# Self attention of a perceiver block: a loop of four heads at a time, or sixteen heads written out with scores three heads ahead

## The chip, the cores and the metric

The kernel runs on one core of one Trainium2 chip, in one launch. The metric is the device time of the whole kernel in microseconds (us), the median of several executions. Engines are named as the profile names them: PE is TensorE's matrix multiplication and PEld its weight load, DVE is VectorE, ACT is ScalarE, POOL is GpSimd, SP is SyncE, which here only issues DMAs.

## The reference, cut to what matters

The whole program is two layers of cross attention, self attention and a feed forward part. The change touches only one piece, the self attention inside the first layer's cross attention block: 256 tokens, 16 query heads of 128, and 8 groups of keys and values, so that two neighbouring query heads share one group. In the reference's own words:

```python
def _gqa(q, k, v):
    scale = 1.0 / np.sqrt(q.shape[-1])
    scores = jnp.einsum('bsghd,btgd->bghst', q, k) * scale
    p = jax.nn.softmax(scores, axis=-1)
    return jnp.einsum('bghst,btgd->bsghd', p, v)
```

The result is divided by a smoothing vector and clipped to the range of fp8 before it goes on to the output projection.

## The kernel before

The kernel is a row of stages. Each stage is one block in which every engine runs its own list of instructions, ordered against the others by semaphores, and every stage ends with a barrier of all engines. `front_stage` computes queries, keys and values, `self_attention_stage` (line 166) is the one that is changed, and `wide_cross_attention_stage` (line 285) follows it. The queries `qT` [128 dims, 16 heads, 256 tokens], keys `kT` [128, 8, 256] and values `v` [128 tokens, 2, 8 x 128] lie in SBUF when the stage begins. All are fp32.

The stage before is a hardware loop of four passes; a pass takes two groups, which is four heads (n = 0 to 3). Per head the work is:

- PE: scores, two products of 128x256 (line 226), then four transposes of 128x128 of the probabilities (line 233), then the weighing of the values, two products of 128x256 into `out` (line 217, function `weigh`). The profile has two records for each fp32 product, so scores and weighing have four records of 128x256 each, and the transposes four of 128x128.
- DVE: the row peaks of the scores (`tensor_reduce`, line 267), the shift (line 268); later the reciprocal of the row sums (line 271) and two multiplications that normalise `prob` (lines 272 and 273); for each group of two heads the outputs are scaled (line 278) and clipped into `cat` (line 280).
- ACT: two exponentials with their sums (line 250), and later the copy of the transposed probabilities out of PSUM (line 255).
- POOL: for each group it copies the queries, keys and values to `q`, `k`, `val` (lines 202 to 204); PE's scores wait for that copy (`s_in`).

A pass runs phase by phase: PE makes the scores of all four heads; DVE finds the four peaks, then normalises the four; ACT makes all eight exponentials, then the four copies; PE turns head n and then weighs head n-1; DVE puts the two groups away at the end. `scores` and `prob` have four buffers each, `tp` two, `out` two. `Chain.after` (called `link`) makes an engine wait until the instruction just issued has completed; it stands behind the first multiplication (line 272) and behind the clipping (line 280) as well.

SP issues five loads for the next stage at the start of this one (lines 3079 and 3081); PE first waits for them in the next stage.

Of the kernel before, what the change touches and what calls it, by code (L numbers as in the profile page):

```python
# [31 lines left out]
NH = 16  # L32
NG = 8
EPS = 1e-5
FP8_MAX = 448.0
# [129 lines left out]

def self_attention_stage(nc, C, qT, kT, v, inv_smooth, cat, loads):

    scale = D**-0.5
    with Stage(nc, "self") as st:
        q = [st.sb(f"q{e}", [P, 2, TOK]) for e in range(2)]
        k = [st.sb(f"k{e}", [P, TOK]) for e in range(2)]
        val = [st.sb(f"val{e}", [P, NT, D]) for e in range(2)]
# [10 lines left out]
        names = "free staged scores shift exp norm turned probT out put dve"  # L186
        s_free, s_in, s_sc, s_sh, s_exp, s_norm, s_tp, s_pt, s_out, s_put, s_dve = (st.sem(n) for n in names.split())
        with nc.Block() as block:

            @block.sync  # L190
            def _(sp):
                loads(sp)

            @block.gpsimd
            def _(pool):

                with pool.Fori(0, NG // 2) as i:
                    for e in range(2):
                        pool.wait_ge(s_out, i * 4 + (2 * e + 2))
                        pool.sem_inc(s_free, 1)  # L200
                        pool.wait_ge(s_free, i * 2 + (e + 1))
                        pool.tensor_copy(q[e][:, :, :], qT[:, bass.ds(i * 4 + 2 * e, 2), :]).then_inc(s_in, 1)
                        pool.tensor_copy(k[e][:, :], kT[:, bass.ds(i * 2 + e, 1), :].rearrange("p a n -> p (a n)")).then_inc(s_in, 1)
                        pool.tensor_copy(val[e][:, :, :], v[:, :, bass.ds(i * (2 * D) + e * D, D)]).then_inc(s_in, 1)

            @block.tensor
            def _(pe):
                pe.sem_inc(s_out, 4)
                pe.sem_inc(s_tp, 4)
                with pe.Fori(0, NG // 2) as i:  # L210
                    def weigh(n):
                        e, u = n // 2, n % 2
                        pe.wait_ge(s_pt, i * 4 + (n + 5))
                        if u == 0:
                            pe.wait_ge(s_put, i * 2 + (e + 1))
                        for kt in range(NT):
                            mm = pe.matmul(out[e][:, u, :], val[e][:, kt, :], probT[n][:, kt, :], start=(kt == 0), stop=(kt == 1))
                        mm.then_inc(s_out, 1)

                    for n in range(4):  # L220
                        e, u = n // 2, n % 2
                        if u == 0:
                            pe.wait_ge(s_in, i * 6 + (3 * e + 3))
                        pe.wait_ge(s_exp, i * 8 + (2 * n + 2))
                        for t in range(NT):
                            mm = pe.matmul(scores[n][:, t, :], q[e][:, u, t * P:(t + 1) * P], k[e][:, :], start=True, stop=True)
                        mm.then_inc(s_sc, 1)
                    for n in range(4):
                        pe.wait_ge(s_norm, i * 4 + (n + 5))
                        pe.wait_ge(s_pt, i * 4 + (n + 3))  # L230
                        for t in range(NT):
                            for kt in range(NT):
                                mm = pe.transpose(tp[n % 2][:, kt, t * P:(t + 1) * P], prob[n][:, t, kt * P:(kt + 1) * P],
                                                  C["ident"][:, :])
                        mm.then_inc(s_tp, 1)
                        if n >= 1:
                            weigh(n - 1)
                    weigh(3)

            @block.scalar  # L240
            def _(act):
                act.sem_inc(s_exp, 8)
                act.sem_inc(s_pt, 4)
                with act.Fori(0, NG // 2) as i:
                    for n in range(4):
                        act.wait_ge(s_tp, i * 4 + (n + 1))
                        act.wait_ge(s_norm, i * 4 + (n + 1))
                        act.wait_ge(s_sh, i * 4 + (n + 1))
                        for t in range(NT):
                            act.activation(prob[n][:, t, :], scores[n][:, t, :], ACT.Exp, bias=shift[:, n, t:t + 1],  # L250
                                           scale=scale, accum_out=total[:, n, t:t + 1]).then_inc(s_exp, 1)
                    for n in range(4):
                        act.wait_ge(s_tp, i * 4 + (n + 5))
                        act.wait_ge(s_out, i * 4 + (n + 1))
                        act.copy(probT[n][:, :, :], tp[n % 2][:, :, :]).then_inc(s_pt, 1)

            @block.vector
            def _(dve):
                PER = 4 * 3 + 2 * 2
                dve.sem_inc(s_norm, 4)  # L260
                dve.sem_inc(s_put, 2)
                with dve.Fori(0, NG // 2) as i:
                    chain = Chain(dve, s_dve, i * PER)
                    link = chain.after
                    for n in range(4):
                        dve.wait_ge(s_sc, i * 4 + (n + 1))
                        link(dve.tensor_reduce(peak[:, n, :], scores[n][:, :, :], AX.X, ALU.max))
                        dve.tensor_scalar(shift[:, n, :], peak[:, n, :], -scale, None, ALU.mult).then_inc(s_sh, 1)
                    for n in range(4):
                        dve.wait_ge(s_exp, i * 8 + (2 * n + 10))  # L270
                        link(dve.reciprocal(inv[:, n, :], total[:, n, :]))
                        link(dve.tensor_scalar(prob[n][:, 0, :], prob[n][:, 0, :], inv[:, n, 0:1], None, ALU.mult))
                        dve.tensor_scalar(prob[n][:, 1, :], prob[n][:, 1, :], inv[:, n, 1:2], None, ALU.mult) \
                           .then_inc(s_norm, 1)
                    for e in range(2):
                        heads = bass.ds(i * 4 + 2 * e, 2)
                        dve.wait_ge(s_out, i * 4 + (2 * e + 6))
                        link(dve.tensor_tensor(scaled[e][:, :, :], out[e][:, :, :],
                                               inv_smooth[:, heads].unsqueeze(2).to_broadcast([P, 2, TOK]), ALU.mult))
                        link(dve.tensor_scalar(cat[:, heads, :], scaled[e][:, :, :], FP8_MAX, -FP8_MAX, ALU.min, ALU.max))  # L280
                        dve.sem_inc(s_put, 1)
                    assert chain.n == PER, chain.n


def wide_cross_attention_stage(nc, C, ctxT, s_ctx, w, s_w, wkv_dram, q_dram, vecs, inv_smooth, cat, units, early):
# [2818 lines left out]
```

## Time and profile before

| | us |
|---|---|
| median of 3 runs | 2563.33 (2561.7 to 2565.37) |
| the profiled execution's own time | 2560.87 |
| its span, first to last instruction | 2559.1 |
| self attention stage, first load issued to last output put | 131.27 to 193.98 |

The span is what the trace covers; the 1.8 us between it and the execution's time lie around it. The stage is 62.7 us, some 2.4% of the span. The mean granted TensorE clock over the whole execution is 0.959 of full speed.

### The profile page before, as it was taken

Reading aid. Unit: us, or ns where it says so; the run is one execution under the profiler, and the core shown is the slowest. Engines: PE = TensorE matmul, PEld = TensorE weight load, DVE = VectorE, ACT = ScalarE, POOL = GpSimd, SP = SyncE. Lnnn points to the kernel's source line nnn. Section 1 sums busy time; section 2 is a strip of 40 time slices with the busy share of each in tenths; the row PEclk is TensorE's granted clock in tenths of the full one; section 3 lists DMA queues with packets and bytes.
Section 4 is the critical chain, followed back from the end, with each engine's and each line's share of the span. In section 5 each row is a group of like instructions: output and inputs, shape, how many; then the busy total and the mean of one; then the engine's idle time right before and its main releaser. Section 6 shows DMA issues by size and latency. Waiting matters only on the chain. (4 is left out here: it accounts for less than half of the span.)

```text
span 2559.1 us, 31520 instructions
## 1 busy us (share of the span) xinstructions
PE 2279.3 (89%) x11472; PEld 1554.3 (61%) x11472; DVE 1786.6 (70%) x3422; ACT 1193.7 (47%) x1924; POOL 587.4 (23%) x435
## 2 busy tenths in 40 slices
PE   3779999999999999896897989788888779899998
PEld 2556666666666666564674456555556337677876
DVE  7856887777777778876896976666767754554444
ACT  4443466666566666633332114576766853211111
POOL 7810033334233333440000003323141300000000
PEclk9889999999999999998997999999999989899999
DMA  3331100000000100003544100000000013656661
GB/s 132 116 140 46 46 25 29 9 29 9 29 25 13 29 13 17 0 1 132 193 169 188 52 21 10 1 10 1 6 5 1 21 75 144 216 206 220 230 237 66
DMA packets 47622, 186.40 MB, mean 73 GB/s; under 512 B 6064, under 2 KB 10928, under 8 KB 37232
## 3 DMA queue, kind: packets, MB, share of 16 engines
q1 hardware_dynamic: 47472, 184.43, 20.0%
q8 instruction: 91, 1.49, 0.2%
q14 instruction: 59, 0.48, 0.1%
HBM read 174.71 MB, written 9.70 MB: 72 GB/s over the span
## 5 line engine op out<-in xcount | busy, mean ns | idle before, releaser
L406 PE MATMUL wide_a<-wide_w,ctxT 128*128 128x256 f32 (+1 forms) x2048 | 437.8, 367 | 2.8 <-POOL wide_eps L375 2.8
L406 PEld LDWEIGHTS wide_a<-wide_w,ctxT 128*128 128x128 f32 x2048 | 368.5, 191 | 76.5 <-issue 35.7
L388 POOL TENSOR_TENSOR wide_sums<-wide_sums,wide_s 128x512 f32<-128x512 f32 x224 | 301.3, 1345 | 461.8 <-ACT wide_s L536 448.6
L431 PE MATMUL wide_scores<-wide_q,wide_keysT 128*128 128x512 f32 x512 | 238.4, 604 | 12.5 <-ACT wide_s L532 12.5
L441 PE MATMUL wide_o<-wide_s,wide_values 128*128 128x512 f32 x512 | 233.8, 600 | 3.5 <-ACT wide_s L536 3.5
L532 ACT COPY wide_s<-wide_scores 128x512 f32<-128x512 f32 x256 | 148.4, 585 | 175.7 <-PE wide_scores L431 173.9
L1812 DVE TENSOR_REDUCE int_peaks<-int_a 128x1 f32<-128x1024 f32 x128 | 156.1, 1222 | 91.3 <-PE int_a L1535 90.1
L1535 PE MATMUL int_a<-int_keys,int_qrows 96*128 96x512 bf16 x512 | 151.8, 394 | 55.9 <-DVE int_peaks L1812 27.9
L1687 ACT ACTIVATE int_prob<-int_a,int_shift,int_qscale 128x1024 uint8<-128x1024 f32 x128 | 155.4, 1216 | 50.6 <-PE int_a L1535 50.1
L431 PEld LDWEIGHTS wide_scores<-wide_q,wide_keysT 128*128 128x128 f32 x512 | 87.9, 189 | 148.8 <-ACT wide_s L532 87.8
L594 DVE TENSOR_TENSOR wide_top<-wide_top,wide_s 128x512 f32<-128x512 f32 x240 | 165.6, 690 | 16.1 <-ACT wide_s L532 10.4
L2268 PEld LDWEIGHTS moe_bank<-moe_xb,moe_gate_up 128*128 128x128 f32 (+1 forms) x1536 | 162.0, 183 | 8.3 <-issue 8.3
L2268 PE MATMUL moe_bank<-moe_xb,moe_gate_up 128*128 128x96 f32 (+1 forms) x1536 | 162.6, 266 | 4.3 <-issue 4.3
L441 PEld LDWEIGHTS wide_o<-wide_s,wide_values 128*128 128x128 f32 x512 | 96.7, 192 | 100.2 <-issue 93.9
L607 DVE TENSOR_TENSOR wide_s<-wide_s,wide_peak_rows 128x2048 f32<-128x2048 f32 x64 | 146.8, 2294 | 0.8
L570 DVE BATCH_NORM_STATS2 wide_stats<-wide_keys 128x6 f32<-128x128 f32 x256 | 60.6, 278 | 110.9 <-ACT wide_values L514 108.4
L1446 PE MATMUL int_vp<-int_wk,ctxT_again 128*128 128x128 f32 x1024 | 126.6, 279 | 5.2 <-PEq L79 2.2
L1446 PEld LDWEIGHTS int_vp<-int_wk,ctxT_again 128*128 128x128 f32 x1024 | 122.7, 194 | 12.3 <-issue 4.0
L512 ACT COPY wide_keys<-wide_a 128x256 f32<-128x256 f32 x128 | 46.6, 364 | 174.3 <-PE wide_a L406 174.2
L536 ACT ACTIVATE wide_s<-wide_s 128x2048 f32<-128x2048 f32 x64 | 122.4, 1912 | 5.5 <-DVE wide_s L607 4.8
L1535 PEld LDWEIGHTS int_a<-int_keys,int_qrows 96*128 96x128 bf16 x512 | 37.0, 99 | 118.8 <-DVE int_peaks L1812 49.7
L2469 DVE TENSOR_REDUCE moe_coef<-moe_misc 96x1 f32<-96x4 f32 x32 | 5.1, 158 | 137.3 <-PE moe_misc L2277 137.3
(425 smaller groups left out, 4285.7 us busy)
## 6 DMA issues: line engine op xcount, KB each, us to landing
moe_gate_up<-hbm_m_gu SPq DMA_DIRECT2D x34, 1408.0 KB, 6.2
moe_down<-hbm_m_down_a SPq DMA_DIRECT2D x34, 512.0 KB, 6.9
causal_wqkv<-hbm_wqkv SPq DMA_DIRECT2D x8, 1536.0 KB, 6.6
ctxT<-hbm_ctxT SPq DMA_DIRECT2D x4, 2048.0 KB, 15.1
oproj_raw<-hbm_wproj SPq DMA_DIRECT2D x8, 1024.0 KB, 5.0
ctxT_again<-hbm_ctxT SPq DMA_DIRECT2D x4, 2048.0 KB, 21.6
wide_unit<-hbm_ffn_units SPq DMA_DIRECT2D x27, 256.0 KB, 2.7
ffn_early<-wide_unit SPq DMA_DIRECT2D x27, 256.0 KB, 2.0
```

Source lines behind the costliest of these rows:

```text
L388: ins = pool.tensor_tensor(sums[0][:, :], before, part[:, j, :], ALU.add)
L406: mm = pe.matmul(a[h][:, j, cols], ctxT[:, kc, t * P:(t + 1) * P], w[g % 2][:, kc, cols], start=(kc == 0), stop=(kc == KC - 1))
L431: pe.matmul(sp_[j % 2][:, :], keysT[:, j, :], q[:, :], start=True, stop=True).then_inc(s_s, 1)
L441: mm = pe.matmul(o[g % 2][:, :], values[m % VR][:, j, :], s[m % SR][:, j, :], start=(c == 0 and j == 0), stop=(c == QPG - 1 and j == 3))
L532: act.copy(s[n % SR][:, j, :], sp_[j % 2][:, :]).then_inc(s_se, 1)
L594: link(dve.tensor_tensor(top[:, :], before, s[n % SR][:, j, :], ALU.max))
L607: dve.tensor_tensor(s[m % SR][:, :, :], s[m % SR][:, :, :], peak_rows[:, :].unsqueeze(1).to_broadcast([P, 4, COLS]), ALU.subtract).then_in ...
L1446: mm = pe.matmul(vp[:, t * P:(t + 1) * P], ctxT[:, kc, i * P:(i + 1) * P], wk[:, kc, :], start=(kc == 0), stop=(kc == KC - 1))
L1535: mm = pe.matmul(wide[n % 2][:, z * 512:(z + 1) * 512], qrows[0:3 * HD, h, t * P:(t + 1) * P], keys[0:3 * HD, h % HC, j * 512:(j + 1) * 51 ...
L1687: act.activation(prob[u % 4][:, p * 1024:(p + 1) * 1024], wide[n % 2][:, :], ACT.Exp, bias=shift[:, u % NU:u % NU + 1], scale=qscale[:, t, ...
L1812: dve.tensor_reduce(peaks[u % 2][:, p:p + 1], wide[n % 2][:, :], AX.X, ALU.max).then_inc(s_ad, 1)
L2268: mm = pe.matmul(dst[0:m, j, :], wgu[i][:, kc, z * EI + f0:z * EI + f0 + m], xb[q % 2][:, kc, e % BATCH, :], start=(kc == 0), stop=(kc == ...
```

## The change

The loop is gone: the sixteen heads are written out (n = 0 to 15), each with its own instructions, so that PE reads `qT`, `kT` and `v` where they are. POOL has no work in the stage. The order on the engines is another one. `AHEAD` is 3: the scores, peaks and exponentials of heads 0 to 2 come first, and then sixteen steps follow. In step n PE turns head n, makes the scores of head n+3 and weighs head n-1; ACT copies the turned head n and makes the exponentials of head n+3; DVE normalises head n, finds the peaks of head n+3, and in every second step from n = 3 puts one group away. Buffers are the same in number. The waits behind the first multiplication and behind the clipping are gone.

```diff
             @block.tensor
             def _(pe):
...
+                for n in range(AHEAD):
+                    score(n)
+                for n in range(NH):
+                    turn(n)
+                    if n + AHEAD < NH:
+                        score(n + AHEAD)
+                    if n >= 1:
+                        weigh(n - 1)
+                weigh(NH - 1)
...
+                def score(n):
+                    if n >= 4:
+                        pe.wait_ge(s_exp, 2 * (n - 3))
+                    for t in range(NT):
+                        mm = pe.matmul(scores[n % 4][:, t, :], qT[:, n, t * P:(t + 1) * P], kT[:, n // 2, :], start=True, stop=True)
+                    mm.then_inc(s_sc, 1)
+
+                def turn(n):
+                    pe.wait_ge(s_norm, n + 1)
+                    if n >= 2:
+                        pe.wait_ge(s_pt, n - 1)
...
+                def weigh(n):
+                    g, u = divmod(n, 2)
+                    pe.wait_ge(s_pt, n + 1)
+                    if u == 0 and g >= 2:
+                        pe.wait_ge(s_put, g - 1)
+                    for kt in range(NT):
+                        mm = pe.matmul(out[g % 2][:, u, :], v[:, kt, g * D:(g + 1) * D], probT[n % 4][:, kt, :],
+                                       start=(kt == 0), stop=(kt == NT - 1))
+                    mm.then_inc(s_out, 1)
...
             @block.scalar
             def _(act):
...
+                for n in range(AHEAD):
+                    exponential(n)
+                for n in range(NH):
+                    keep_turned(n)
+                    if n + AHEAD < NH:
+                        exponential(n + AHEAD)
...
             @block.vector
             def _(dve):
...
+                def find_peak(n):
+                    dve.wait_ge(s_sc, n + 1)
+                    link(dve.tensor_reduce(peak[:, n % 4, :], scores[n % 4][:, :, :], AX.X, ALU.max))
+                    dve.tensor_scalar(shift[:, n % 4, :], peak[:, n % 4, :], -scale, None, ALU.mult).then_inc(s_sh, 1)
+
+                def normalise(n):
+                    dve.wait_ge(s_exp, 2 * n + 2)
+                    link(dve.reciprocal(inv[:, n % 4, :], total[:, n % 4, :]))
+                    dve.tensor_scalar(prob[n % 4][:, 0, :], prob[n % 4][:, 0, :], inv[:, n % 4, 0:1], None, ALU.mult)
+                    dve.tensor_scalar(prob[n % 4][:, 1, :], prob[n % 4][:, 1, :], inv[:, n % 4, 1:2], None, ALU.mult).then_inc(s_norm, 1)
+
+                def put(g):
+                    heads = slice(2 * g, 2 * g + 2)
+                    dve.wait_ge(s_out, 2 * g + 2)
+                    link(dve.tensor_tensor(scaled[g % 2][:, :, :], out[g % 2][:, :, :],
+                                           inv_smooth[:, heads].unsqueeze(2).to_broadcast([P, 2, TOK]), ALU.mult))
+                    dve.tensor_scalar(cat[:, heads, :], scaled[g % 2][:, :, :], FP8_MAX, -FP8_MAX, ALU.min, ALU.max).then_inc(s_put, 1)
+
+                for n in range(AHEAD):
+                    find_peak(n)
+                for n in range(NH):
+                    normalise(n)
+                    if n + AHEAD < NH:
+                        find_peak(n + AHEAD)
+                    if n >= 3 and n % 2 == 1:
+                        put((n - 3) // 2)
+                put(NG - 1)
```

## Rows read from the trace of the kernel before

**Rows 1.** Windows, a pass each: length; PE, PEld, DVE, ACT, POOL busy; clock; DMA share; GB/s
```profile
131.30:146.00 14.70, 10.02 (x51) 8.02 (x52) 8.08 (x23) 7.17 (x21) 4.03 (x10) 1.00 0.94 389
146.00:161.60 15.60, 12.58 (x50) 9.53 (x49) 9.14 (x25) 7.22 (x21) 2.98 (x6) 0.78 0.48 205
161.60:177.20 15.60, 11.95 (x47) 9.21 (x46) 9.00 (x24) 7.17 (x21) 2.98 (x6) 0.78 0.00 1
177.20:194.00 16.80, 11.68 (x50) 8.70 (x48) 10.12 (x26) 7.17 (x21) 1.49 (x3) 0.90 0.00 0
```

**Rows 2.** Waits within 131.3 to 194.1 us: waiter, releaser, total us, times, longest
```profile
ACT L250 <- DVE self_shift L268: 17.9, 4, 4.9
...
PE self_tp L233 <- DVE self_prob L273: 10.3, 7, 2.6
...
PE self_scores L226 <- POOL self_val L204: 4.1, 4, 3.5
```

**Rows 3.** Timeline of the first pass: start us, us, engine, line, operation, idle before
```profile
131.27 0.33 SPq L3079 DMA_DIRECT2D wide_w<-hbm_wkvx  x1
...
133.19 3.72 PE L226 MATMUL self_scores<-self_k,self_q 128*128 128x256 f32 x16 [3.48 <-POOL self_val L204]
...
134.35 0.69 DVE L267 TENSOR_REDUCE self_peak<-self_scores 128x2 f32<-128x512 f32 x1 [9.54 <-PE self_scores L226]
135.08 0.17 DVE L268 TENSOR_SCALAR self_shift<-self_peak 128x2 f32<-128x2 f32 x1
...
135.35 1.28 ACT L250 ACT_TABLE_LOAD   x1 [4.92 <-DVE self_shift L268]
...
137.67 0.17 DVE L268 TENSOR_SCALAR self_shift<-self_peak 128x2 f32<-128x2 f32 x1
137.77 0.17 DVE L271 RECIPROCAL self_inv<-self_total 128x2 f32<-128x2 f32 x1
...
137.97 0.35 DVE L272 TENSOR_SCALAR self_prob<-self_prob,self_inv 128x256 f32<-128x256 f32 x1
...
138.36 0.35 DVE L273 TENSOR_SCALAR self_prob<-self_prob,self_inv 128x256 f32<-128x256 f32 x1
...
138.85 0.65 PE L233 MATMUL self_tp<-ident,self_prob 128*128 128x128 f32 x4 [1.94 <-DVE self_prob L273]
```

**Rows 4.** Timeline later in that pass, and the outputs put away beside it
```profile
142.40 1.03 PE L217 MATMUL self_out<-self_probT,self_val 128*128 128x256 f32 x4
...
143.27 0.60 PE L233 MATMUL self_tp<-ident,self_prob 128*128 128x128 f32 x4
...
143.70 1.97 PE L217 MATMUL self_out<-self_probT,self_val 128*128 128x256 f32 x8
...
145.81 0.69 DVE L278 TENSOR_TENSOR self_scaled_out<-self_out,inv_smooth 128x512 f32<-128x512 f32 x1 [0.80 <-PE self_out L217]
...
146.65 0.58 DVE L280 TENSOR_SCALAR cat<-self_scaled_out 128x512 f32 x1 [0.15 <-DVE self_scaled_out L278]
```

**Rows 5.** Timeline of the second pass, behind its idle stretch on PE
```profile
152.19 2.02 PE L233 MATMUL self_tp<-ident,self_prob 128*128 128x128 f32 x8 [2.58 <-DVE self_prob L273]
...
154.42 2.07 PE L217 MATMUL self_out<-self_probT,self_val 128*128 128x256 f32 x4 [0.21 <-ACT self_probT L255]
...
156.28 1.06 PE L233 MATMUL self_tp<-ident,self_prob 128*128 128x128 f32 x4
...
157.14 1.92 PE L217 MATMUL self_out<-self_probT,self_val 128*128 128x256 f32 x4
```

**Rows 6.** Timeline: the last output, and the first products of the next stage
```profile
193.55 0.43 DVE L280 TENSOR_SCALAR cat<-self_scaled_out 128x512 f32 x1 [0.15 <-DVE self_scaled_out L278]
...
195.34 9.91 PE L406 MATMUL wide_a<-wide_w,ctxT 128*128 128x256 f32 x37 [2.77 <-POOL wide_eps L375]
```

**Rows 7.** Timeline, next stage: four multiplications with no wait between them
```profile
214.06 1.12 DVE L582 TENSOR_SCALAR wide_keys<-wide_keys,wide_mv,wide_rstd 128x128 f32<-128x128 f32 x4
```

**Rows 8.** Groups by line, VectorE, 205 to 330 us: busy, mean ns, idle before
```profile
L582 DVE TENSOR_SCALAR wide_keys<-wide_keys,wide_mv,wide_rstd 128x128 f32<-128x128 f32 x44 | 12.3, 341 | 0.4
```

More of the change, by code:

```diff
@@ L171, in self_attention_stage @@
     scale = D**-0.5
+    AHEAD = 3
     with Stage(nc, "self") as st:
-        q = [st.sb(f"q{e}", [P, 2, TOK]) for e in range(2)]
-        k = [st.sb(f"k{e}", [P, TOK]) for e in range(2)]
-        val = [st.sb(f"val{e}", [P, NT, D]) for e in range(2)]
         prob = [st.sb(f"prob{n}", [P, NT, TOK]) for n in range(4)]
@@ L185, in self_attention_stage @@
         out = [st.ps(f"out{e}", [P, 2, TOK]) for e in range(2)]
-        names = "free staged scores shift exp norm turned probT out put dve"
-        s_free, s_in, s_sc, s_sh, s_exp, s_norm, s_tp, s_pt, s_out, s_put, s_dve = (st.sem(n) for n in names.split())
+        names = "scores shift exp norm turned probT out put dve"
+        s_sc, s_sh, s_exp, s_norm, s_tp, s_pt, s_out, s_put, s_dve = (st.sem(n) for n in names.split())
         with nc.Block() as block:
@@ L192, in _ @@
                 loads(sp)
[L194 to L204, printed above, removed]
@@ L206, in _ @@
             @block.tensor
             def _(pe):
[L208 to L215, printed above, removed]
-                        for kt in range(NT):
[L217 to L238, printed above, removed]
@@ new lines, in score @@
+                def score(n):
[8 more added lines that the diff above has]
+                        pe.wait_ge(s_pt, n - 1)
+                    for t in range(NT):
+                        for kt in range(NT):
+                            mm = pe.transpose(tp[n % 2][:, kt, t * P:(t + 1) * P], prob[n % 4][:, t, kt * P:(kt + 1) * P],
+                                              C["ident"][:, :])
+                    mm.then_inc(s_tp, 1)
@@ L240, in _, with exponential @@
+                for n in range(NH):
[5 more added lines that the diff above has]
+                weigh(NH - 1)
             @block.scalar
             def _(act):
[L242 to L255, printed above, removed]
+                def exponential(n):
+                    act.wait_ge(s_sh, n + 1)
+                    if n >= 4:
+                        act.wait_ge(s_tp, n - 3)
+                    for t in range(NT):
+                        act.activation(prob[n % 4][:, t, :], scores[n % 4][:, t, :], ACT.Exp, bias=shift[:, n % 4, t:t + 1],
+                                       scale=scale, accum_out=total[:, n % 4, t:t + 1]).then_inc(s_exp, 1)
@@ L257, in _, with keep_turned @@
+                def keep_turned(n):
+                    act.wait_ge(s_tp, n + 1)
+                    if n >= 4:
+                        act.wait_ge(s_out, n - 3)
+                    act.copy(probT[n % 4][:, :, :], tp[n % 2][:, :, :]).then_inc(s_pt, 1)
+                for n in range(AHEAD):
[4 more added lines that the diff above has]
+                        exponential(n + AHEAD)
             @block.vector
@@ L258, in _ @@
             def _(dve):
[L259 to L282, printed above, removed]
@@ new lines, in _ @@
+                link = Chain(dve, s_dve).after
+                def find_peak(n):
[7 more added lines that the diff above has]
+                    dve.tensor_scalar(prob[n % 4][:, 1, :], prob[n % 4][:, 1, :], inv[:, n % 4, 1:2], None, ALU.mult).then_inc(s_norm, 1)
```

## The prediction

> **What bounds the kernel now.** Only one stage of 62.7 us changes, from the first load at 131.27 [rows 3] to the last output's end at 193.55 + 0.43 = 193.98 [rows 6]; everything else can only be shifted. First I read the windows, one for each pass of the loop [rows 1]: in none of the four is an engine busy all the time (PE 10.0 to 12.6 us of passes of 14.7 to 16.8 us, DVE 8.1 to 10.1, ACT 7.2). So no engine is the bound; a chain of waits through all of them is. Then the waits [rows 2]: ACT waits 17.9 us for the first shift of each pass, PE 10.3 us for normalised probabilities, PE 4.1 us for GpSimd's copies. The timeline of the first pass shows the chain [rows 3]: scores at 133.19, the first peak at 134.35, the shift at 135.08, then a table load of 1.28 us on ACT behind it, the exponentials, the reciprocal at 137.77, two multiplications, and the first transposes at 138.85, PE having idled for 1.94 us. Later in the pass PE runs dense: four records of weighing, then four transposes 0.87 us later, then the next weighing 0.43 us later [rows 4]. The clock column [rows 1] is 1.00 in the first pass, 0.78, 0.78 and 0.90 in the others. With two levels, 2.4 and 1.2 GHz, that is (1 - 0.78) x 2 x 15.6 = 6.9 us at the low one, again 6.9, and (1 - 0.90) x 2 x 16.8 = 3.4, 5.7 on the mean. The falls lie around the idle stretch before the transposes, 2.58 us in the second pass [rows 5] (this row stands for three, of 2.55 to 2.58), not around the 1.94 us of the first [rows 3]. PE also idled 2.77 us at the border to the next stage [rows 6].
>
> **What the change removes.** GpSimd's copies: scores can start at the stage's start, about 131.5 (I take 0.2 behind the first load at 131.27) in place of 133.19, 1.7 us earlier, and the smaller waits for later copies go, 0.2 each. Three of four table loads should go, as one load served both exponentials and copies within a pass and the list is now one; each stood between a shift and an exponential [rows 3], 3 x 1.28 = 3.8 us. The borders between passes go, where PE has no softmax work to turn. These gains aren't added to anything below: the new stage is summed from its start, and they are inside it.
>
> **What it adds: a closed loop through PE and DVE.** Read the new lists in order. DVE: normalise(n), peak(n+3), normalise(n+1). PE: turn(n), score(n+3), weigh(n-1). turn(n) waits for normalise(n); score(n+3) is queued behind it on PE; peak(n+3) waits for the scores; normalise(n+1) is queued behind the peak on DVE. So though the exponentials are three heads ahead, no step can be shorter than this round:
> - end of normalising to first transpose 0.14 (138.36 + 0.35 to 138.85 [rows 3])
> - transposes to what follows on PE 0.43 (143.27 to 143.70 [rows 4])
> - start of the scores to start of the peak 1.16 (133.19 to 134.35 [rows 3])
> - peak to shift 0.73, shift to reciprocal 0.10, reciprocal to first multiplication 0.20 [rows 3]
> - first multiplication to second: 0.39 before, with a wait between them [rows 3]. The wait is gone. Four multiplications of half the size with no wait take 1.12 us [rows 7] where one takes 0.341 [rows 8], so the next starts (1.12 - 0.341) / 3 = 0.26 after the one before, 0.08 less than its length. The same here: 0.35 - 0.08 = 0.27, call it 0.28. Bounds: 0.28 and 0.39
> - second multiplication 0.35 [rows 3]
>
> Sum 3.39 us. In every second step from n = 3 a put stands between peak(n+3) and normalise(n+1): 0.84 from scaling to clipping (145.81 to 146.65), and the clipping, 0.58 beside GpSimd's copies [rows 4] and 0.43 without them [rows 6], less the overlap of 0.08: about 1.20. A long step is 4.59. ACT, with 7.2 / 4 = 1.8 us a head [rows 1], and PE's weighing, 0.87 [rows 4], fit under either. The Trainium skill speaks on the wait taken out: "VectorE: DVE Perf Modes", section "The DRAIN you can't avoid", says that leaving semaphores out between VectorE operations saves nothing. By that each step would be 0.11 longer, 1.4 us over 13 steps; rows 7 and 8 show the overlap, and I go by them.
>
> **The sum.** From score(0) at 131.5 to the first reciprocal it takes what it took, 137.77 - 133.19 = 4.58, the one table load in it: 136.1. Thirteen steps (n = 0 to 12) have the round: 13 x 3.39 = 44.1, and five puts among them (n = 3, 5, 7, 9, 11) add 6.0: 186.2. The tail has no scores: normalise(13) 0.83, put 1.20, normalise(14) 0.83, normalise(15) meanwhile; turn(14) starts at 189.2 and ends its 0.43, weigh(13) 0.87, turn(15) 0.43, to 190.9; the copy of head 15 runs to 191.8 beside weigh(14); weigh(15) 1.03 to 192.9; 0.13 more, then put(7), 0.84 + 0.43: the end at 194.3. Before it was 193.98. At full clock the change is worth +0.3 us: the borders, copies and loads saved are spent again on the round, (13 x 3.39 + 6.0) / 13 = 3.9 us a head, the same as the 15.6 / 4 = 3.9 of a pass [rows 1].
>
> **The clock on top.** In a short step PE works 0.43 + 0.87 + 0.87 = 2.17 and idles 1.2 us; in a long one it idles 2.4. That is between the 1.94 us that left the clock up and the 2.55 that brought it down each time, and there are five long steps. At the low level the transposes' 0.43 becomes 0.86 (156.28 to 157.14 [rows 5]) and the scores' four records 2.07 [rows 5] in place of 1.03 [rows 4]; both lie in the round, so a step is 1.47 longer, 4.86. A fall that holds 5.7 us, the mean of before, costs 5.7 x 1.47 / 4.86 = 1.7 us. Before, falls met short transposes alone behind the idle stretch; here 2.17 us of work follow each gap, so I take two falls of five: 3.4. Total +3.7 us. Bounds: none, and all steps low, 13 x 1.47 = 19.1.
>
> **At nothing.** SP's five loads for the next stage are issued as before, now with no wait of PE for them until the next stage; its first product is at 195.34 [rows 6]. Reading `qT`, `kT`, `v` in place: same shapes and types, 0. Straight code on PE is four times as long as the loop's body and is fetched while those loads fill the DMA engines (share 0.94 [rows 1]); nothing here shows a price, I bound it by 0 and by one step, 3.4, and take 0. Weighing one head later is covered: its copy of 0.6 us is made long before.
>
> **Rivals.**
> A (forecast): few falls of the clock, +3.7: the profiled execution's 2560.87 becomes 2564.6, and the median, 2563.33 or 2.46 above it, 2567.0. Own range +1.5 to +6.
> B: the clock falls at each long step. 5 x 1.7 = 8.6, plus 0.3: +8.9, 2572.2. For it: the gaps of 2.4 us, near 2.55. Against: in pass one, gap 1.94, nothing fell. The Trainium skill, "Perfetto Trace Analysis", section "Matmul Optimizations", would have this rival: the engine scales its power by use, so matmuls should run back to back in batches, and the change spreads batches of eight and sixteen into small ones. The trace bears it out only where idle stretches were over 2.5 us.
> C: no fall; the new stage is as long as the old, +0.3: 2563.6. The pipeline is there, but the round eats it.
> D (the other side): the round is not closed, that is, DVE finds the scores of head n+3 ready whenever it comes to them. Then DVE is free of the 0.14 + 0.43 + 1.16, and PE's own 2.17 or DVE's 0.73 + 0.10 + 0.83 + 0.60 (half a put) = 2.26 binds: 13 x (3.85 - 2.26) = 20.7 us less, 2543. It needs scores issued ahead of the wait for normalise(n), and the list has them behind it. It decides from a saving of 5.4 / 13 = 0.4 us a step.
>
> **The numbers.** 0.2% of 2563 is 5.1 us, about what a measurement of this kernel can tell from no change. A 0.50, B 0.25, C 0.17, D 0.08. Slower by over 0.2%: nearly all of B (0.23) and the upper end of A (0.05), 0.28. Faster: 0.07 from D. Within: 0.65. The range is 2561 to 2573: C's lower side (if the fixed hops are some 0.2 us shorter a step) to just above B; it leaves out D and the steps all at low clock. The time is A's, 2567.0; A's own range is 2564.8 to 2569.3.
>
> **What would show it.** In the profile after: DVE waiting for scores (line of the peak) 13 times, 1.7 us or so each, and PE waiting for the normalised probabilities 13 times; starts of the peaks 3.4 and 4.6 us apart by turns; one table load in the stage; no GpSimd work; the clock between 0.85 and 1.00. Wrong if the peaks come 2.3 us apart (D), if PE waits for nothing between steps, if steps at full clock are not near 3.39, or if the clock is under 0.8 (B).

## The result, and the profile after

The changed kernel takes 2552.63 us (median of 9 runs, 2550.07 to 2554.79) where the kernel before takes 2561.7 (9 runs): a ratio of 0.9970, 95% interval 0.9959 to 0.9981, some 7.7 us or 0.3% faster. One of the nine executions of the kernel before took 9195.4 us and is left out of the ratio, which goes by the median of the other eight, 2560.4. The forecast was 2567.0 in 2561 to 2573, no measurable change most likely. The time lies below the range and the sign of the likeliest case was wrong.

The page of the changed kernel begins:

```profile
span 2550.8 us, 31191 instructions
...
PE 2268.6 (89%) x11472; PEld 1546.6 (61%) x11472; DVE 1783.5 (70%) x3422; ACT 1191.7 (47%) x1921; POOL 575.8 (23%) x411
```

The windows of the stage in four stretches, columns as in [rows 1]; the stage runs from 130.08 to 189.40 us:

```profile
130.08:145.00 14.92, 9.79 (x49) 7.60 (x50) 7.83 (x24) 8.94 (x28) 0.00 (x0) 1.00 0.95 392
145.00:160.00 15.00, 9.51 (x49) 7.29 (x49) 8.22 (x24) 6.42 (x20) 0.00 (x0) 1.00 0.49 206
160.00:175.00 15.00, 10.50 (x45) 7.64 (x43) 8.13 (x24) 6.00 (x19) 0.00 (x0) 0.89 0.00 1
175.00:189.40 14.40, 10.05 (x52) 7.63 (x52) 8.84 (x25) 5.40 (x15) 0.00 (x0) 1.00 0.00 0
```

GpSimd is idle, and the clock is down in one stretch only: (1 - 0.89) x 2 x 15.0 = 3.3 us, against 6.9 + 6.9 + 3.4 in [rows 1]. PE's busy time for the same 192 records fell from 46.2 to 39.9 us, mostly for that reason. The stage fell from 62.71 to 59.32 us. The waits within it (in the form of [rows 2]):

```profile
DVE self_peak L257 <- PE self_scores L195: 29.4, 14, 7.7
...
PE self_tp L204 <- DVE self_prob L264: 18.2, 14, 1.9
ACT self_prob L235 <- DVE self_shift L258: 17.2, 14, 1.9
```

This is the closed round: VectorE waited 14 times for scores, PE 14 times for normalised probabilities; the three heads of lead take nothing off this round. The start of the stage, which answers to [rows 3]:

```profile
130.08 0.33 SPq L3078 DMA_DIRECT2D wide_w<-hbm_wkvx  x1
130.08 1.28 ACT L235 ACT_TABLE_LOAD   x1 [0.85 <-PEq L79]
...
130.12 2.83 PE L195 MATMUL self_scores<-kT,qT 128*128 128x256 f32 x12 [1.61 <-PEq L79]
...
131.26 0.69 DVE L257 TENSOR_REDUCE self_peak<-self_scores 128x2 f32<-128x512 f32 x1 [7.66 <-PE self_scores L195]
...
133.71 0.17 DVE L258 TENSOR_SCALAR self_shift<-self_peak 128x2 f32<-128x2 f32 x1
133.79 0.16 DVE L262 RECIPROCAL self_inv<-self_total 128x2 f32<-128x2 f32 x1
```

The table load now lies at the very start, before ACT waits for the first shift. VectorE finds three peaks in front of the first reciprocal, where the loop has four [rows 3], and the reciprocal is 3.67 us behind the first score, not 4.58. One step with a put, from the turning of head 3 to that of head 4 (it answers to [rows 3, 4]):

```profile
144.33 0.65 PE L204 MATMUL self_tp<-ident,self_prob 128*128 128x128 f32 x4 [0.84 <-DVE self_prob L264]
...
144.82 1.03 PE L195 MATMUL self_scores<-kT,qT 128*128 128x256 f32 x4
...
145.89 0.69 DVE L257 TENSOR_REDUCE self_peak<-self_scores 128x2 f32<-128x512 f32 x1 [1.61 <-PE self_scores L195]
146.62 0.17 DVE L258 TENSOR_SCALAR self_shift<-self_peak 128x2 f32<-128x2 f32 x1
146.69 0.68 DVE L269 TENSOR_TENSOR self_scaled_out<-self_out,inv_smooth 128x512 f32<-128x512 f32 x1
```

```profile
147.41 0.43 DVE L271 TENSOR_SCALAR cat<-self_scaled_out 128x512 bf16<-128x512 f32 x1
147.75 0.16 DVE L262 RECIPROCAL self_inv<-self_total 128x2 f32<-128x2 f32 x1
147.95 0.35 DVE L263 TENSOR_SCALAR self_prob<-self_prob,self_inv 128x256 f32<-128x256 f32 x1
148.22 0.35 DVE L264 TENSOR_SCALAR self_prob<-self_prob,self_inv 128x256 f32<-128x256 f32 x1
```

```profile
148.62 0.66 PE L204 MATMUL self_tp<-ident,self_prob 128*128 128x128 f32 x4 [1.90 <-DVE self_prob L264]
```

The first and the last of these three fences are the timeline of all engines, the middle one that of VectorE alone, which keeps the clipping apart. The step is 148.62 - 144.33 = 4.29 us; without a put it is 3.23 (peaks at 136.21, 139.44, 142.66 and 145.89).

### The profile page after: what moved, and what is told of

It is laid out like the page before. It is cut to its first block and busy times, and to the rows that moved or that the text cites. A ratio compares the mean times of both kernels' runs of the same rounds, so it can differ in the third digit from the quotient of the medians.

```text
span 2550.8 us, 31191 instructions
## 1 busy us (share of the span) xinstructions
PE 2268.6 (89%) x11472; PEld 1546.6 (61%) x11472; DVE 1783.5 (70%) x3422; ACT 1191.7 (47%) x1921; POOL 575.8 (23%) x411
## 5 line engine op out<-in xcount | busy, mean ns | idle before, releaser
L1445 PEld LDWEIGHTS int_vp<-int_wk,ctxT_again 128*128 128x128 f32 x1024 | 124.0, 195 | 13.1 <-issue 4.3
## 6 DMA issues: line engine op xcount, KB each, us to landing
ctxT_again<-hbm_ctxT SPq DMA_DIRECT2D x4, 2048.0 KB, 20.7
```

Source lines behind the costliest of these rows:

```text
L1445: mm = pe.matmul(vp[:, t * P:(t + 1) * P], ctxT[:, kc, i * P:(i + 1) * P], wk[:, kc, :], start=(kc == 0), stop=(kc == KC - 1))
```

## The experiments

"Stage" is from the first load of the stage to the end of its last output in the profiled execution, as 62.71 us before. "Clock" is the granted clock's mean in that stretch. Each ratio from control on is to executions of the kernel before taken beside it (medians 2559.76 to 2560.1). Below, a "hop" is the time from one engine's work to the work on another that waited for it.

| kernel | median us | ratio to before, 95% interval | stage us | clock |
|---|---|---|---|---|
| before | 2561.7 | | 62.71 | 0.86 |
| changed | 2552.63 | 0.9970 (0.9959 to 0.9981) | 59.32 | 0.97 |
| control | 2559.80 | 0.9997 (0.9987 to 1.0007) | 64.91 | 0.79 |
| before_third | 2556.00 | 0.9991 (0.9976 to 1.0005) | 63.87 | 0.81 |
| after_again | 2551.61 | 0.9971 (0.9960 to 0.9981) | 59.32 | 0.97 |
| u_place | 2547.49 | 0.9952 (0.9938 to 0.9967) | 52.84 | 0.90 |
| u_pool | 2549.44 | 0.9958 (0.9945 to 0.9972) | 57.79 | 0.85 |
| loop_warm | 2554.47 | 0.9980 (0.9970 to 0.9990) | 58.30 | 0.88 |
| links | 2554.47 | 0.9980 (0.9971 to 0.9988) | 63.63 | 0.95 |
| ahead2 | 2554.64 | 0.9985 (0.9973 to 0.9996) | 61.27 | 0.97 |
| put_early | 2544.84 | 0.9951 (0.9934 to 0.9968) | 53.26 | 1.00 |
| open_loop | 2538.34 | 0.9913 (0.9899 to 0.9928) | 42.46 | 1.00 |
| open_put_early | 2530.62 | 0.9890 (0.9874 to 0.9907) | 38.92 | 1.00 |
| u_place_long | 2552.20 | 0.9972 (0.9960 to 0.9983) | 58.22 with the added copies | 0.89 |

**control: the kernel before, unchanged.**

> The kernel before, run again and profiled once more, to see what its profile repeats. Theory 1 (the gain outside the stage is chance: TensorE's clock falls at other places from run to run): the stage from first load to last output is again 61 to 64 us, while the stages before and after it differ from the first profile by one to several us, about as much as the changed kernel's did (1.2 us before the stage, some 3.6 us after it). Theory 2 (the change shortens other stages as well): the rest of the kernel repeats within 0.5 us. Ratio to the kernel before 1.000, within 0.2%, by both.

The stage took 64.91 us. In front of it nothing changed (first load at 131.20, 131.27 before); behind it, from the next stage's first product to the end, it took 2562.0 - 197.47 = 2364.5 us, 2363.8 before, 0.7 apart. This one profile nearly fits the second theory, so the question went on to before_third and u_place_long.

**u_place: the old order, written out, read in place.** Each `Fori` becomes a Python loop, and GpSimd's block goes.

```diff
-                with pe.Fori(0, NG // 2) as i:
+                for i in range(NG // 2):
...
-                            mm = pe.matmul(scores[n][:, t, :], q[e][:, u, t * P:(t + 1) * P], k[e][:, :], start=True, stop=True)
+                            mm = pe.matmul(scores[n][:, t, :], qT[:, 4 * i + n, t * P:(t + 1) * P], kT[:, 2 * i + e, :], start=True, stop=True)
```

> The old order, phase by phase in passes of four heads, but written out without a loop, with constant waits, and with queries, keys and values read in place. Theory 1 (what gained is the loop's disappearance: table loads inside it, register arithmetic and waits against registers, GpSimd's copies): the stage falls to 50 to 57 us from 62.7, as much as or more than the change's 59.3, and the whole kernel is 5 to 12 us faster than before. Theory 2 (the new order gained, through less idle TensorE and a clock that stays up): the stage stays at 60 us or more and the kernel is within 3 us of before.

The stage fell to 52.84 us, 6.5 below the changed kernel's, and the kernel is 12.3 us faster than before against the change's 7.7 (its slowest execution, 2549.55, is below the changed kernel's fastest, 2550.07). So the new order did not bring the gain: writing out and reading in place did, and the new order gave part of it back. The windows of the whole stage:

```profile
129.77:182.61 52.84, 42.22 (x192) 33.51 (x192) 34.32 (x96) 25.45 (x81) 0.00 (x0) 0.90 0.41 170
```

And one hop of it from VectorE to PE, normalising to turning:

```profile
148.67 0.35 DVE L256 TENSOR_SCALAR self_prob<-self_prob,self_inv 128x256 f32<-128x256 f32 x1
...
149.08 0.66 PE L216 MATMUL self_tp<-ident,self_prob 128*128 128x128 f32 x4 [2.06 <-DVE self_prob L256]
```

From 148.67 + 0.35 = 149.02 to 149.08 is 0.06 us, where the loop has 0.14 [rows 3]. The same is seen in u_pool, and the scaling of an output is 0.73 us ahead of its clipping in both, 0.84 in the loop [rows 4]; loop_warm, which keeps the loop, keeps 0.13 and 0.84. The work is the same in u_pool, so these two places cost 0.08 and 0.11 us more in the loop. That registers in its waits and addresses are what costs is likely, but no run separates it.

**u_pool: the same, GpSimd's copies kept.**

> The kernel before, written out without a loop, with constant waits, but GpSimd still copies queries, keys and values. Theory (the loop itself costs, the copies only at their start and a little in each pass): the stage is 54 to 56 us, 1.5 to 3 us above u_place's 52.8. Rival (the copies are what cost, the loop is free): the stage stays at 60 us or more, 7 us or more above u_place.

57.79 us, 4.9 above u_place, more than expected. 3.05 us of it is the start: PE, kept waiting for the first copies, began 1.3 us later, and the clock fell 1.1 us behind its start, for 3.4 us.

```profile
132.10 5.41 PE L226 MATMUL self_scores<-self_k,self_q 128*128 128x256 f32 x16 [3.24 <-POOL self_val L204]
```

Sixteen records of scores took 5.41 us, 3.72 in [rows 3]; the first reciprocal came 7.92 us behind the first load, 4.87 in u_place. The passes afterwards are as long as u_place's (the first reciprocals of two passes are 13.1 to 13.5 us apart in both). Another 1.7 us came behind the last of these, where the clock fell once more and in u_place did not. Against before, writing out alone gave 10.7 us of kernel time, of which the profiled stages show 6.0 against the mean of before's three (63.8).

**loop_warm: the loop kept, the table load moved.**

```diff
                 with act.Fori(0, NG // 2) as i:
+                    act.activation(warm[:, :], C["ident"][:, 0:1], ACT.Exp)
```

> The kernel before with its loop, and one exponential of a single column of the identity into an unused tile at the start of each pass on ACT, so that the table load is done while ACT has nothing else to do, not between the first shift and the first exponential. Theory (the load of 1.28 us stands on the path of each pass, and the idle stretch of TensorE that it lengthens brings the clock down): the load leaves the path, 4 x 1.28 = 5 us off the stage of 62.7 to 64.9, and the idle stretches of 2.55 us before the first transposes of a pass become 1.3, so that the clock falls less often, 1 to 3 us more. Rival (the load is hidden behind something else): no change.

```profile
145.06 1.28 ACT L246 ACT_TABLE_LOAD   x1
146.36 0.20 ACT L246 ACTIVATE self_warm<-ident 128x1 f32<-128x1 f32 x1
149.34 0.47 ACT L252 ACTIVATE self_prob<-self_scores,self_shift 128x256 f32<-128x256 f32 x1 [2.78 <-DVE self_shift L270]
```

The load lies behind the copies of the pass before. The stage is 58.30 us and the kernel 5.1 us faster (interval 2.6 to 7.7): one small instruction in the old loop brings two thirds of what the whole change brought. But the load did not cost its 1.28 us in each pass, as expected. First reciprocals of the first two passes here, a stretch at full clock:

```profile
139.08 0.17 DVE L273 RECIPROCAL self_inv<-self_total 128x2 f32<-128x2 f32 x1
...
151.63 0.17 DVE L273 RECIPROCAL self_inv<-self_total 128x2 f32<-128x2 f32 x1
```

The pass took 12.55 us, against 13.35 at full clock in the kernel before (137.77 [rows 3] to 151.12): 0.80 us, 3.2 over four passes, which is an estimate. The first reciprocal of a pass did not come earlier; in both kernels it stands right behind the fourth shift, 5.56 and 5.61 us behind the second pass's first scores. What came earlier is what follows the exponentials on ACT: in the first pass the first copy of turned probabilities started 0.69 us behind the start of its transposes, not 1.40, and PE's weighing waits for it. The other 1.2 of the 4.4 us between the two profiled stages are not traced; the clock was 0.88 here, 0.86 there. The second half of the expectation failed too: PE's idle stretches were still 1.94 and 2.50 to 2.54 us.

**links: the two waits put back.**

```diff
-                    dve.tensor_scalar(prob[n % 4][:, 0, :], prob[n % 4][:, 0, :], inv[:, n % 4, 0:1], None, ALU.mult)
+                    link(dve.tensor_scalar(prob[n % 4][:, 0, :], prob[n % 4][:, 0, :], inv[:, n % 4, 0:1], None, ALU.mult))
```

(and the same behind the clipping, which then signals by an instruction of its own, as before the change)

> The changed kernel with the two waits put back, behind the first normalising multiplication and behind the clipping. Theory (the trace's overlap of VectorE instructions with no wait between them is real): each step is 0.12 us longer (second multiplication 0.39 behind the first, not 0.27) and each of the puts 0.1 to 0.15, in all 2 to 2.5 us on a stage of 59.3. Rival (leaving such waits out saves nothing): the steps stay at 3.23 and 4.29.

VectorE's timeline in a step with a put:

```profile
144.86 0.35 DVE L263 TENSOR_SCALAR self_prob<-self_prob,self_inv 128x256 f32<-128x256 f32 x1
145.25 0.35 DVE L264 TENSOR_SCALAR self_prob<-self_prob,self_inv 128x256 f32<-128x256 f32 x1
...
148.74 0.43 DVE L271 TENSOR_SCALAR cat<-self_scaled_out 128x512 bf16<-128x512 f32 x1
149.31 0.17 DVE L262 RECIPROCAL self_inv<-self_total 128x2 f32<-128x2 f32 x1
```

The multiplications are 0.39 us apart, 0.27 without the wait, and the reciprocal 0.57 behind the clipping, 0.34 without it (147.41 to 147.75 above). Steps are 3.35 and 4.64 us at full clock: over thirteen steps with five puts 13 x 0.12 + 5 x 0.23 = 2.7 us. The kernel is 2.4 us slower than the mean of the changed one's two medians (2552.1), though the two intervals overlap; the timeline is the firmer evidence. The profiled stage, 63.63, also has one fall of the clock more in it than the changed kernel's.

**ahead2: AHEAD = 2.**

> The changed kernel with scores, peaks and exponentials two heads ahead in place of three. Theory of the closed round: how far ahead the scores are makes no difference to a step, it is 3.23 us again; there is one more step with scores (14) and one head fewer in front of them, so the stage is within 2 us of the changed kernel's. Rival (the distance hides ACT's exponentials and matters): steps become longer by a good part of the two exponentials, 0.5 us or more each, and the kernel 6 us or more slower than the changed one.

```profile
135.87 0.69 DVE L257 TENSOR_REDUCE self_peak<-self_scores 128x2 f32<-128x512 f32 x1 [1.61 <-PE self_scores L195]
...
139.09 0.69 DVE L257 TENSOR_REDUCE self_peak<-self_scores 128x2 f32<-128x512 f32 x1 [1.61 <-PE self_scores L195]
```

Steps are 3.23 us again and the stage 61.27, 2.0 above. The lead of three heads does not set the step. With two peaks in front of the first reciprocal it came 3.12 us behind the first score, and waited 0.22 us for an exponential.

**open_loop: scores ahead of the turning.**

```diff
                 for n in range(NH):
-                    turn(n)
                     if n + AHEAD < NH:
                         score(n + AHEAD)
+                    turn(n)
```

> The changed kernel with one edit: in each step TensorE issues the scores of head n+3 before it turns head n, so they no longer stand behind the wait for normalise(n). Theory of the closed round (as in the prediction): VectorE no longer waits for scores, steps fall from 3.23 and 4.29 us to TensorE's own work, about 2.25 on the mean, so the 13 steps take 29 to 31 us in place of 48, the stage 41 to 45 us, and the kernel is 14 to 18 us faster than the changed one. Rival (the steps are bound by something else, ACT's exponentials or VectorE's own work with its latencies): steps stay above 3 us on the mean and the gain is under 4 us.

The stage fell by 16.9 us to 42.46 and the kernel by 13.8 below the changed kernel's mean median, a little less than expected. Two steps take 5.15 us together, 2.58 each, not 2.25. Why not less shows in the timeline:

```profile
150.95 0.69 DVE L257 TENSOR_REDUCE self_peak<-self_scores 128x2 f32<-128x512 f32 x1 [0.96 <-PE self_scores L195]
...
151.75 0.68 DVE L269 TENSOR_TENSOR self_scaled_out<-self_out,inv_smooth 128x512 f32<-128x512 f32 x1
...
153.68 0.66 PE L204 MATMUL self_tp<-ident,self_prob 128*128 128x128 f32 x4 [0.60 <-DVE self_prob L264]
```

In the step with a put VectorE first waits 0.96 us for scores, then does the put, and PE waits 0.60 us for the probabilities behind it.

**put_early: the put ahead of the peaks.**

```diff
                     normalise(n)
+                    if n >= 3 and n % 2 == 1:
+                        put((n - 3) // 2)
                     if n + AHEAD < NH:
                         find_peak(n + AHEAD)
-                    if n >= 3 and n % 2 == 1:
-                        put((n - 3) // 2)
```

> The changed kernel with one edit: in the steps that have a put, VectorE does it before it looks for the peaks of head n+3, not after. Theory of the closed round: VectorE waits 1.6 us for those scores in each step anyway, the put of 1.06 us goes into that wait, and all steps are 3.23 us; the five long steps of 4.29 vanish, which takes 5 us off the stage (59.3 to 54) and off the kernel. Rival (VectorE's own work is the bound): the order of its work makes no difference, steps stay 3.23 and 4.29.

```profile
141.51 0.69 DVE L257 TENSOR_REDUCE self_peak<-self_scores 128x2 f32<-128x512 f32 x1 [1.62 <-PE self_scores L195]
...
143.03 0.68 DVE L269 TENSOR_TENSOR self_scaled_out<-self_out,inv_smooth 128x512 f32<-128x512 f32 x1
143.75 0.43 DVE L271 TENSOR_SCALAR cat<-self_scaled_out 128x512 bf16<-128x512 f32 x1
144.73 0.69 DVE L257 TENSOR_REDUCE self_peak<-self_scores 128x2 f32<-128x512 f32 x1 [0.56 <-PE self_scores L195]
...
147.96 0.69 DVE L257 TENSOR_REDUCE self_peak<-self_scores 128x2 f32<-128x512 f32 x1 [1.61 <-PE self_scores L195]
```

The put lies in the wait, 0.56 us of which is left; every step is 3.23 us, also the one with the put. The stage is 53.26 us and the kernel 7.3 us below the changed kernel's mean median. Swapping two calls on VectorE is worth as much as the whole change.

**open_put_early: both.**

> Both edits: scores of head n+3 before the turning of head n on TensorE, and the put before the peaks on VectorE. In open_loop a pair of steps takes 5.15 us, and in it VectorE still waits 0.96 us for scores, while its put makes TensorE wait for normalised probabilities. Theory: the put fills that wait, and a pair comes down to TensorE's own work, 2 x 2.2 = 4.4 us; the stage falls from 42.5 to 38 or 39 us, the kernel by 3 to 4 us below open_loop. Rival (the latencies from peaks through exponentials to the normalising bind now): the pair stays at 5.15.

```profile
128.85:167.77 38.92, 36.35 (x192) 29.68 (x192) 32.45 (x96) 26.02 (x81) 0.00 (x0) 1.00 0.56 230
```

PE is busy 36.35 of 38.92 us at full clock. Steps are 2.58 and 1.75 or 1.92 us, a pair 4.33 to 4.50: now PE is the bound. The stage fell by 3.5 us below open_loop's, as expected; the kernel's medians differ by 7.7, more than expected, from five executions each. The kernel is 2530.62 us, 1.1% (0.9 to 1.3%) faster than before and the fastest of all, 21 us ahead of the change.

**after_again and before_third.**

> The changed kernel once more, for a second profile and time. Theory (the fixed hops decide, the clock adds by chance): at full clock the steps are again 3.23 and 4.29 us to 0.02, and what differs is the number of falls of the clock in the stage, 0 to 4, each some 0.8 to 1.5 us; the stage is 58.6 to 64 us and the kernel 5 to 9 us faster than before. Rival (the first profile's single fall is a property of this order): the stage is again 59.3 within 0.3.

> The kernel before, profiled a third time, for the spread of its stages. The stage 61 to 65 us, the stages behind it 2363 to 2366 us if the difference to the written out kernels is a property of the kernel; anywhere in 2357 to 2366 if it is chance.

The changed kernel's stage was 59.32 us once more, with one fall of 3.4 us at another place; its steps at full clock were 3.23 and 4.29. It is what the rival had said; but links and ahead2, with the same order, had two falls and one, so how many come is not settled by two equal profiles. The kernel before had 63.87 us, and behind the stage 2554.1 - 195.80 = 2358.3 us, among what the written out kernels showed. So the stages behind differ by 6 us from one execution to another of one program.

**u_place_long.**

```diff
+                for r in range(12):
+                    link(dve.tensor_copy(scaled[0][:, :, :], scaled[1][:, :, :]))
```

> u_place with twelve copies of 128x512 on VectorE behind its last output, each waited for, about 0.6 to 0.8 us each: nothing of it is used, it only makes the stage as long as the looped kernel's. The stages behind the self attention took 2363.7 to 2366.0 us in three looped profiles and 2357.1 to 2362.3 in seven written out. Theory (that is the time of day: the later stages meet other falls of TensorE's clock when they start earlier): with the stage 7 to 10 us longer they take 2363 to 2366 again, and the kernel is 3 us or more slower than u_place plus the added stage time. Rival (it is the code: straight lists in place of loops change something that lasts): they stay at 2357 to 2362, and the kernel is u_place's time plus the added stage time.

A copy took 0.46 us, so the stage grew by only 5.6 us, from 52.58 without the copies. The kernel became 4.7 us slower, no more than the added time, and behind the stage it took 2550.9 - 189.88 = 2361.0 us. That speaks against the theory of the starting time, weakly, since the added time was smaller than meant. The same profile has a pass of the old order, written out, at full clock:

```profile
136.91 0.16 DVE L254 RECIPROCAL self_inv<-self_total 128x2 f32<-128x2 f32 x1
...
148.43 0.16 DVE L254 RECIPROCAL self_inv<-self_total 128x2 f32<-128x2 f32 x1
```

It took 11.52 us, 2.88 us a head.

## Why the prediction was wrong

**Right: the round.** PE and VectorE form one closed chain, at full clock every step has the length of that chain, a step with a put is longer by the put, and the lead of three heads hides nothing of it. open_loop and put_early, each an exchange of two calls, break it as the theory says, and ahead2 leaves it alone. Read in this order, the head costs 47.3 / 13 = 3.64 us at full clock (forecast 3.85).

**Wrong: the sum of the stage, 66.4 us (63.0 at full clock and 3.4 for the clock), measured 59.32.** Term by term:

| term | forecast | measured | difference |
|---|---|---|---|
| first load to first reciprocal | 4.83 | 3.71 | -1.1 |
| 13 rounds | 13 x 3.39 | 13 x 3.23 | -2.1 |
| 5 puts in them | 5 x 1.20 | 5 x 1.06 | -0.7 |
| tail | 8.1 | 7.6 | -0.5 |
| low clock | 3.4 | 0.75 | -2.7 |

So the steps that failed are, by size, the hops in the rounds and puts (2.8 us), the two long falls of the clock (2.7) and the start that was to take what it took (1.1).

The first reciprocal: "it takes what it took, the one table load in it" was wrong twice. Two chains ended there together in the kernel before: the four peaks, behind which the fourth shift started at 137.67 [rows 3], and the load with the first head's exponentials on ACT, whose sums were done at 137.67:

```profile
137.47 0.20 ACT L250 ACTIVATION_READ_ACCUMULATOR self_prob<-self_scores,self_shift 128x1 f32 x1
```

The new order has three peaks there, 0.86 us less, and the load moved ahead of the wait for the shift; either alone would have left the other chain in the way: in loop_warm, with the load early and four peaks, the first reciprocal still stands 0.11 us behind the fourth shift. (In u_place, written out too, the load stayed behind the shift, at 132.25 us with the shift at 131.97, and four peaks made it 4.53 us; what places the load isn't shown by the traces.) Scores also started 0.04 us behind the first load, not 0.2.

In the rounds, normalised to turned was 0.05, not 0.14, and scaling to clipping in a put 0.72, not 0.84; u_pool and u_place show that this belongs to writing out, not to the order. Scores to peak was 1.07, not 1.16, and that does not: I had read it at the first products of a stage, where u_place has 1.14, u_pool 1.17 and the changed kernel 1.14 too, and its rounds have 1.07. Shift to reciprocal was 0.08, not 0.10. Transposes to scores was longer, 0.49, not 0.43: I had read it in PE's dense stretch, where four transposes take 0.60 us, and behind an idle stretch they took 0.65 already before [rows 3]. I had no bounds for hops: I had bounded only what the trace of before did not show and took what it showed as a property of the engine.

**The clock.** I gave the new stage falls as long as the old one's, 5.7 us, two of them. One of 3.4 us came, in both profiles. The cost of low clock was sized a little high (two steps of 3.87 and 4.40 in place of 3.23 and 4.29, 0.75 us for 3.4 us at the low level, 1.0 by the forecast's rate; no step was low as a whole). The error is in how many falls come and how long they hold. PE's idle stretch in a long step was 1.90 us, not 2.4: the step was 0.30 us shorter, and PE's own work in it is 2.39 us, not 2.17, since the last product's end had been left out:

```profile
163.65 0.66 PE L204 MATMUL self_tp<-ident,self_prob 128*128 128x128 f32 x4 [1.90 <-DVE self_prob L264]
...
164.14 1.68 PE L195 MATMUL self_scores<-kT,qT 128*128 128x256 f32 x4
```

Scores took 1.68 us there, as the clock fell within them. The premise that 1.94 us of idling leave the clock up, and only some 2.55 bring it down, came from one profile and does not hold. In control, behind the same stretch:

```profile
141.43 0.67 PE L233 MATMUL self_tp<-ident,self_prob 128*128 128x128 f32 x4 [1.94 <-DVE self_prob L273]
...
142.28 1.11 PE L233 MATMUL self_tp<-ident,self_prob 128*128 128x128 f32 x4 [0.18 <-DVE self_prob L273]
```

Four transposes of 1.11 us are at the low level; before_third shows the same fall. The low clock took up 17 us of the stage in the first profile of before, 27 in control and 24 in before_third.

The larger oversight is on the other side: the comparison was with a stage that itself pays for its falls. First reciprocals of the passes of the kernel before, the first at 137.77 [rows 3]:

```profile
151.12 0.17 DVE L271 RECIPROCAL self_inv<-self_total 128x2 f32<-128x2 f32 x1
...
166.72 0.17 DVE L271 RECIPROCAL self_inv<-self_total 128x2 f32<-128x2 f32 x1
```

The pass at full clock took 151.12 - 137.77 = 13.35 us, the next, with 6.9 us at the low level, 15.60. At 13.35 / 4 = 3.34 us a head the old loop, at full clock, is faster than the new order's 3.64, and the old order written out, 2.88 in u_place_long, is faster still. The forecast's "the same as the 15.6 / 4 = 3.9 of a pass" had set steps at full clock beside a pass with 6.9 us at the low level. The falls cost the second and third passes (15.60 and 16.23 us) 2.25 and 2.88 us over 13.35, so at full clock the old stage would have been 57.6 us or less, the new one 59.32 - 0.75 = 58.6; these are estimates. What the change gained in the stage, 3.4 us here and 4.5 on the mean of the three profiles before (63.8), is less than what the falls cost the old stage; against the old loop it came from a clock that stays at 0.97 where it was 0.79 to 0.86. No run held the clock in the old loop to show it alone.

**Why not more.** Writing out and reading in place is worth 12.3 us (u_place). The change includes both, so the rest of it costs 4.6 us against the old order written out, through the round: 3.64 us a head at full clock for 2.88. The two waits that the change takes out are in that rest, and u_place keeps them; as links puts them at 2.4 to 2.7 us, the order alone costs some 7, an estimate. For the order alone the forecast's sign was right; for the change it was not, and no term of the sum was there for what the loop itself costs.

**The rivals.** B (falls at each long step) did not come. The rule of the Trainium skill that stood beside it ("Perfetto Trace Analysis", section "Matmul Optimizations") does not decide this stage: with small batches and gaps of 0.84 and 1.90 us the clock stayed up better (0.97) than with the old order's large batches and gaps of 1.94 to 2.58 (0.79 to 0.86), or of 1.83 to 2.07 written out (0.90). C had the mechanism (the round eats the pipeline) but not the size. D (the round not closed) was right that opening it is worth most: 16.9 us in the stage, where I had put 20.7. On VectorE's waits the Trainium skill ("VectorE: DVE Perf Modes", section "The DRAIN you can't avoid") says that chaining operations without semaphores saves nothing, though it also says that a next operation that is not held starts earlier. The traces show such an earlier start: the two waits cost 2.7 us by the steps of links.

**Open.** The medians differ by 7.4 to 7.7 us, the profiled stages by 4.5 on the mean. The rest, some 3 us, lies in stages whose code is the same. Behind the stage the three profiles before took 2363.8, 2364.5 and 2358.3 us and loop_warm 2366.0, the two after 2360.2 and 2357.5 and the others that are written out 2357.2 to 2362.4; the spread in one program is as large as the difference, so these profiles can't say whether that part belongs to the change. Part of the miss is also the starting point: 2563.33 was the median of three runs, 35 later ones of the kernel before have 2559.98.

## What to carry to other kernels

When work is issued ahead, follow the in-order queue of each engine around once: if the work ahead stands behind a wait of the current item on one engine, and what consumes it stands in front of the next item on the other, the lead is worth nothing and a step is the sum of the round. Put what waits last in the queue and what fills the wait first. Put two versions beside each other at the same clock. And compare with the old code written out in the old order before crediting a new order: durations and hops read from a hardware loop, its table loads included, are not those of straight code.

## What the runs showed of the hardware

- The looped stage has 4 table loads of 1.28 us, one in each pass, every written out one has a single load. In the loop it stood between the wait for the shift and the exponential; with a throwaway exponential at the pass's start a pass at full clock went from 13.35 to 12.55 us, 0.80 less, not 1.28.
- A hop from VectorE to TensorE took 0.05 to 0.06 us with constant waits and 0.13 to 0.14 in the loop.
- The granted clock fell behind an idle stretch of 1.90 us in one step and stayed up behind equal ones in four others of the same execution; behind 1.94 in the first pass of the kernel before it stayed up in one profile and fell in two. The length of the idle stretch alone does not decide.
- In the profiled stages a low stretch lasted 3.4 or 6.8 us. One of 3.4 cost the changed kernel 0.75 us, spread over two steps; at u_pool's start, over scores in a row, the 16 records took 5.41 us, 1.7 more than at full clock.
